# Layer 0's group steps behind their inputs, and norms by a power on GpSimd, in a four-layer graph network kernel

## The reference

```
L0: w = einsum(emb, weight);  out = sum_k T_k(adj) x w_k + emb bias
L1: h' = softmax(mask(adj > 0.5)) h;  out = elu(h')
L2: emb = x W' + b;  out = (adj + I) emb / deg
L3: three times  v = relu([v, adj v] W1' + b1) W2' + b2
x = layernorm(x + out)      # after each of the four
```

## Time and profile before

| | |
|---|---|
| median of 3 runs | 1052.36 us (1052.09 to 1052.92) |
| profiled execution | 1052.66 us, of it the profile's span 1050.9 us |
| PE busy | 1023.4 us (97%) |
| DVE / ACT / POOL busy | 690.4 / 453.4 / 538.1 us (66 / 43 / 51%) |
| granted PE clock | full, but for the last slice of 40 |
| first matmul, last matmul's end | 5.56 us, 1042.3 us |

### The profile page before, as it was taken

How to read it: one execution, slowest core, us unless ns; L and a number is a source line. 1 busy time by engine, 2 the same in 40 slices (tenths; PEclk the granted TensorE clock), 3 DMA queues, 4 the chain that set the end, 5 groups by cost and what they waited for, 6 DMA issues and landing times.

```text
span 1050.9 us, 18768 instructions
## 1 busy us (share of the span) xinstructions
PE 1023.4 (97%) x6922; PEld 490.9 (47%) x6922; DVE 690.4 (66%) x1728; ACT 453.4 (43%) x1097; POOL 538.1 (51%) x625
## 2 busy tenths in 40 slices
PE   7999999999999999999999999999999999999995
PEld 3445444434443444344345555555554545455553
DVE  3876565677547765775674778876546677767556
ACT  4632333333334343534423677557556622132632
POOL 0005486546456766775671757579764232223311
PEclk9999999999999999999999999999999999999998
DMA  9930000000000000000010121212112100000022
GB/s 365 400 128 1 2 1 2 1 2 1 1 1 2 1 1 2 1 1 2 1 41 1 41 81 41 81 41 80 53 69 81 41 1 1 3 2 21 22 61 61
DMA packets 14658, 45.66 MB, mean 43 GB/s; under 512 B 960, under 2 KB 9280, under 8 KB 10080
## 3 DMA queue, kind: packets, MB, share of 16 engines
q1 hardware_dynamic: 14560, 44.39, 11.4%
HBM read 40.19 MB, written 4.19 MB: 42 GB/s over the span
## 4 chain that ended last, share of the span: by engine, by line
PE 84%; DVE 9%; POOL 2%; ACT 2%; DMA 2%; issue 1%; SPq 0%; POOLq 0%; ACTq 0%; DVEq 0%
PE PS L750 34%; PE PS L880 21%; PE PS L924 18%; DMA BW<-at_in 2%; PE PS L735 2%; PE PS L737 2%; PE PS L736 2%; DVE BW L1200 1%; DVE T L1203 1%; DVE X L1203 1%; PE PS L744 1%; PE PS L742 1%; PE PS L743 1%; ACT T L1043 1%; PE PS L725 1%
## 5 line engine op out<-in xcount | busy, mean ns | idle before, releaser
L750 PE MATMUL PS<-BW,S 128*128 128x512 fp8e4 x1792 | 403.5, 379 | 4.3 <-POOL S L1708 1.9
L750 PEld LDWEIGHTS PS<-BW,S 128*128 128x128 f16 x1792 | 169.6, 98 | 211.0 <-issue 15.9
L1043 ACT ACTIVATE T<-PS,SM 128x128 f32<-128x128 f32 x384 | 112.5, 365 | 206.9 <-DVE X L1203 137.7
L880 PE MATMUL PS<-WZ,R 64*128 64x512 f16 x1536 | 198.5, 377 | 3.1 <-ACT T L1043 3.1
L1745 POOL TENSOR_TENSOR T<-T 128x128 f32<-128x128 f32 (+1 forms) x192 | 127.0, 662 | 124.9 <-ACT T L1043 114.4
L1203 DVE SCALAR_TENSOR_TENSOR X<-PS,SM,X 128x128 f32<-128x128 f32 x320 | 109.9, 344 | 38.7 <-PE PS L880 38.5
L880 PEld LDWEIGHTS PS<-WZ,R 64*128 64x128 f16 x1536 | 69.2, 94 | 106.8 <-issue 25.4
L924 PE MATMUL PS<-BW,S 128*128 128x512 fp8e4 x512 | 115.4, 379 | 0.4 <-issue 0.4
L1745 POOL TENSOR_TENSOR S<-R,S 128x512 f16<-128x512 f32 x48 | 57.5, 1210 | 94.2 <-ACT S L1043 94.2
L880 PE MATMUL PS<-WZ,T 64*128 64x512 f16 x768 | 103.8, 376 | 0.0
L1203 DVE SCALAR_TENSOR_TENSOR T<-PS,SM,T 128x128 f32<-128x128 f32 x256 | 88.0, 344 | 21.2 <-PE PS L880 21.2
(11 more groups left out here) (215 smaller groups left out, 1476.9 us busy)
## 6 DMA issues: line engine op xcount, KB each, us to landing
WZ<-a_in SPq DMA_DIRECT2D x16, 1024.0 KB, 4.8
BW<-at_in SPq DMA_DIRECT2D x8, 1024.0 KB, 18.3
R<-at_in SPq DMA_DIRECT2D x7, 1024.0 KB, 13.7
out<-X SPq DMA_DIRECT2D x16, 256.0 KB, 2.3
X<-x_in SPq DMA_DIRECT2D x3, 1024.0 KB, 20.3
T<-w_in SPq DMA_DIRECT2D x1, 1536.0 KB, 16.0
R<-at_in SPq DMA_DIRECT2D x2, 512.0 KB, 5.2
SM<-sm_in SPq DMA_DIRECT2D x1, 520.5 KB, 18.3
```

Of the source, the lines that this page charges most:

```text
L750: m = e.matmul(o, stile(h, t, c), Bm[:, t, block(j)], start=(t == 0 and h == 0), stop=(last and t == NT - 1 and h == 1))
L880: m = e.matmul(bank(b0 + q), halves[kd][zh][r, :], WZ[r, wh, kd, block(g)], start=(i == 0), stop=(i == 8))
L1043: return e.activation(o, i, f, **kw)
```

## The change

It does five things:

1. The group steps are placed by rounds counted through (`g` = 4u + t). `sq` is split into `sq` (ScalarE) and `red` (VectorE), with `red` a round or more behind. There are four buffers for the squares where layers 0 and 1 had one. `mean` goes from the second round of the unit after the group's norm to the second round of the unit after that, `addrow` and all behind it further on, for c = 3 into slots 2 to 11 of the last part (before: 0 to 7). The chains of `scales` are cut into six; two of them (`scales_b`, `scales_c`) go behind the middle.
2. `Z` is two steps, one a group, and on VectorE the low halves of `dx`, `E1`, `E2` and `E` 0 (`lo`) stand between the two groups of the following round. PE's order of `Z`, products, `dx` and `t1` stays.
3. In the head, `xs` 1 goes from before `P1` 2 to behind `t1` 3.
4. The weights' root: no Sqrt on ScalarE; GpSimd takes a maximum and a power of 0.5 right after its reduction over partitions, and VectorE waits for it.
5. The norms: no `var` on VectorE and no Sqrt; GpSimd adds epsilon and takes the power -0.5 of the sums (`var`, `var3`), 32 or 16 columns. `rs` on VectorE is four operations, one refining step, without the reciprocal.

```diff
-        + [("xs", 0), ("xs", 1)]
-        + pieces("P1", 2) + [("t1", 2), ("dx", 3), ("t1", 3), ("E1", 10), ("bounds",), ("xs", 2)]
+        + [("xs", 0)]
+        + pieces("P1", 2) + [("t1", 2), ("dx", 3), ("t1", 3), ("xs", 1), ("E1", 10), ("bounds",), ("xs", 2)]
...
+    for c in range(NC):
+        g = 16 * c
+        for j in range(4):
+            late = (c, j) == (3, 3)
+            at(g + 4 * j + (5 if late else 6), ("sq", 0, c, j))
+            at(g + 4 * j + (6 if late else 7), ("red", 0, c, j))
+        g += 16
+        if c < 3:
+            at(g + 3, ("var", 0, c))
+            at(g + 4, ("rs", 0, c), ("apply", 0, c, 0))
+            for j in (1, 2, 3):
+                at(g + 4 + j, ("apply", 0, c, j))
+            at(g + 7, ("sum", c))
+            g += 9
+            at(g, ("mean", c), ("row_a", c))
+            at(g + 1, ("row_b", c))
+            for j in range(4):
+                at(g + 2 + j, ("addrow", c, j))
+                at(g + 4 + j, ("sq", 1, c, j))
+                at(g + 5 + j, ("red", 1, c, j))
+            at(g + 8, ("var", 1, c))
+            for j in range(4):
+                at(g + 9 + j, *[("rs", 1, c)][j:], ("apply", 1, c, j), ("split", c, j))
...
     for k in range(5):
-        at(k // 2, 1 + 2 * (k % 2), ("xs", 3 + k))
-    at(2, 3, ("scales", 0))
-    at(3, 1, ("scales", 1))
-    at(3, 2, ("scales", 2))
+        at(2 * k + 1, ("xs", 3 + k))
+    at(9, ("scales", 0))
+    at(11, ("scales", 1))
+    at(13, ("scales", 2))
+    at(15, ("scales", 3))
+    at(65, ("scales", 4), ("scales", 5))
...
-            order += [("Z", u, t), ("add", u, t)]
-            order += after.pop((u, t), [])
+                if order[-1][0][0] == "E":
+                    lo.append(("lo", *order[-1]))
+
+            order += [("Z", u, t, 0), *lo, ("Z", u, t, 1), ("add", u, t)]
+            lo = []
+            order += after.pop(4 * u + t, [])
             if c < 3 and j < 2:
                 v = 4 * (c + 1) + 2 * j + t // 2
                 order.append(("dx" if t % 2 == 0 else "t1", v))
-        order += after.pop((u, 4), [])
+                if t % 2 == 0:
+                    lo.append(("lo", *order[-1]))
...
-                elif jt == 10:
-                    e.wait_ge(s_wsqr, 1)
-                    fn(col(cT3), col(cT3), ACT.Sqrt).then_inc(s_wroot, 1)
...
-                    e.wait_ge(s_wroot, 1)
-                    vc(ts(e, col(cZ), col(cT3), 1e-30, 1.0 / 1024, ALU.max, ALU.mult))
+                    e.wait_ge(s_wsqr, 3)
+                    vc(ts(e, col(cZ), col(cT3), 1.0 / 1024, None, ALU.mult))
...
-                    fc(e.reciprocal(s1, s1))
-                    fc(e.tensor_tensor(s0, s1, s1, ALU.mult))
-                    fc(e.tensor_tensor(s0, s0, s2, ALU.mult))
-                    fc(ts(e, s0, s0, -0.5, 1.5, ALU.mult, ALU.add))
-                    e.tensor_tensor(s2, s1, s0, ALU.mult).then_inc(s_rs, 1)
+                    m, eps = norm_scale(L)
+                    fc(e.tensor_tensor(s2, s1, s1, ALU.mult))
+                    fc(stt(e, s2, s0, eps, s2, ALU.add, ALU.mult))
+                    fc(ts(e, s2, s2, -0.5 * m ** 0.5, 1.5 * m ** 0.5, ALU.mult, ALU.add))
+                    e.tensor_tensor(s2, s1, s2, ALU.mult).then_inc(s_rs, 1)
...
             e.partition_all_reduce(col(cT3), wst[:, 0:1], 128, RED.max).then_inc(s_wsqr, 1)
+            e.wait_ge(s_wsqr, 1)
+            e.tensor_scalar(col(cT3), col(cT3), 1e-36, None, ALU.max).then_inc(s_wsqr, 1)
+            e.wait_ge(s_wsqr, 2)
+            e.tensor_tensor(col(cT3), col(cT3), col(cHalf), ALU.pow).then_inc(s_wsqr, 1)
...
+                elif kind in ("var", "var3"):
...
+                    s0, s1 = (st_part(L, c, j, k, 2 if L == 3 else 1) for k in range(2))
+                    pc(e.tensor_scalar(s1, s0, norm_scale(L)[1], None, ALU.add))
+                    e.tensor_tensor(s1, s1, col(cHalf + 1).broadcast_to(list(s1.shape)), ALU.pow).then_inc(s_pw, 1)
```

More of the change, by code:

```diff
@@ L31 @@
 cSG, cISG, cKG = 36, 40, 44
+cHalf = 46
 cF = 50
@@ L100, in at @@
-    def at(u, t, *steps):
-        after.setdefault((u, t), []).extend(steps)
+    after, rest = {}, {}
+    def at(g, *steps):
+        (after if g < 64 else rest).setdefault(g if g < 64 else g - 64, []).extend(steps)
     for c in range(NC):
+        g = 16 * c
         for j in range(4):
[L105 to L120, removed]
@@ L121, in middle_order @@
-    order = []
-    for k in range(5):
-        at(k // 2, 1 + 2 * (k % 2), ("xs", 3 + k))
-    at(2, 3, ("scales", 0))
-    at(3, 1, ("scales", 1))
-    at(3, 2, ("scales", 2))
+            late = (c, j) == (3, 3)
[18 more added lines that the diff above has]
+                at(g + 9 + j, *[("rs", 1, c)][j:], ("apply", 1, c, j), ("split", c, j))
+        else:
+            at(g + 2, ("var", 0, c))
+            at(g + 3, ("rs", 0, c), ("apply", 0, c, 0), ("apply", 0, c, 1))
+            at(g + 4, ("apply", 0, c, 2), ("apply", 0, c, 3), ("sum", c))
+            at(g + 6, ("mean", c), ("row_a", c))
+            at(g + 7, ("row_b", c))
+            for j in range(4):
+                at(g + 7 + j // 3, ("addrow", c, j))
+                at(g + 8 + j // 3, ("sq", 1, c, j))
+                at(g + 9, ("red", 1, c, j))
+            at(g + 9, ("var", 1, c))
+            for j in range(4):
+                at(g + 10 + j // 2, *[("rs", 1, c)][j:], ("apply", 1, c, j), ("split", c, j))
@@ L156, in at @@
         late.setdefault(k, []).extend(steps)
-    for (u, t) in sorted(after):
-        at(u - 16, *after[u, t])
+    for k in sorted(after):
+        at(k, *after[k])
     for c in range(NC):
@@ L1054, in scalar_steps @@
                     act_e2(e, step[1])
-                elif kind == "scales" and step[1] == 0:
+                elif kind == "scales" and step[1] == 1:
                     e.wait_ge(s_xc, NT)
@@ L1404, in scales_c @@
                 e.wait_ge(s_sc, 1)
-                for t in range(2):
-                    e.wait_ge(s_hh, 2 + t)
-                    stt(e, hat[:, 1, t:4:2, :], BD[:, t::2, :], cs[:, cRho64 + t:cRho64 + t + 1], hat[:, 0, t:4:2, :],
-                        ALU.mult, ALU.subtract).then_inc(s_hl, 1)
             for step in steps:
                 kind = step[0]
-                if kind == "E1":
-                    dve_e1(e, step[1])
+                if kind == "lo" and step[1] == "E1":
+                    dve_e1(e, step[2])
+                elif kind == "lo" and step[1] == "E2":
+                    dve_e2(e, step[2])
+                elif kind == "lo" and step[1] == "dx":
+                    dve_dx(e, step[2])
+                elif kind == "lo":
+                    e.wait_ge(s_zh, 1)
+                    lo_half(e, T[:, 0, 1, block(0)], bank(product_bank(0)), T[:, 0, 0, block(0)], s_zl)
@@ L1524, in vector_steps @@
                     ts(e, ROW[:, 0, :], ROW[:, 0, :], LAM, None, ALU.mult).then_inc(s_row, 1)
-                elif kind == "E":
+                elif kind == "E" and step[1] > 0:
                     k = step[1]
```

193 lines of the change are left out of this document (94 added, 99 removed).

## The result

| kernel | median | range | against before, 95% interval |
|---|---|---|---|
| before, beside it | 1052.82 us | 1052.09 to 1053.16 (5) | |
| changed | 1099.02 us | 1098.08 to 1099.79 (5) | 1.044 [1.0428, 1.0453] |

A forecast was written before the change was run, and what follows sets the result against it. TensorE, busy 97% of the span, was taken to bound the kernel, so only its waits counted. -8.7 + 7.4 - 0.3 + 2.1 + 0.3 = +0.8 on the profiled 1052.66, with the median 0.3 lower: 1053.2 us, range 1046.0 to 1058.5.

The forecast's parts named there:

- part 2: `lo` between a round's two groups: low halves release PSUM banks 0.29 us late for TensorE's next products, +7.4 us.
- part 4: Head: the root by GpSimd's power waits for its code to reload, delaying VectorE and then TensorE, +2.1 us.
- part 5: Norms: power taken as 1.3 us for 32 columns, 0.8 for 16, hidden in the middle, exposed at the end; +0.3 us.
- (d): Rival, norms: the power is slow and decides from 3 us on; 1057.2 at 4 us, near 1070 at 7; chance 0.15.
- Part 1: Group steps placed later in middle and last part: TensorE's seven gaps for ScalarE, VectorE and the mean go, -8.7 us.
- rival (e): Last part: layer 1's later steps meet GpSimd's mask differences and hold back product 12; 2 to 3 us, 1056; chance 0.10.
- 20 to 30: Sign of being right: that many short TensorE waits for VectorE's low halves, 0.1 to 0.2 us idle each.
- Part 3: Head, `xs` 1 later: GpSimd's 1.9 us wait goes, but TensorE waits in the third round; -0.3 us kept.
- The end: After VectorE's last sum, the last norm's power and four operations stand before the output: 1.67 us grows, +0.4 us.

The follow-up runs named there:

- e2: e1 with the `lo` halves ahead of the round again (changed order, roots on ScalarE): 1050.33 us, 0.9975 of the kernel before.
- e1: Changed kernel with its order kept but every root, head and norms, back on ScalarE's Sqrt, no power: 1054.85 us, 1.0023 of the kernel before.
- e11: Changed kernel with only the `lo` halves ahead of the round's first group again; power kept for head and norms: 1094.91 us, 1.0398 of before.
- e3: Changed kernel with only the head's root back on ScalarE; norms keep GpSimd's power: 1095.99 us, 1.0414 of the kernel before.
- e5: e2 plus five unread GpSimd powers of 1 to 64 columns and one multiplication before GpSimd's first all-reduce: 1051.67 us, executed once.
- e6: e2 plus GpSimd powers of the same size at each norm's place, results unread, norms using ScalarE's roots: 1057.22 us, 1.0048 of before.
- e7: Changed kernel with head's root on ScalarE, `lo` halves ahead, groups 0 to 2 one round later from `rs` on: 1086.33 us, 1.0311 of before.
- e9: e2 with layer 1's mean, row, squares and applies of the last column group one slot earlier, one apply per slot: 1048.52 us, 0.9962 of before.
- e12: e9 with the head's `xs` 1 back ahead of the third product's pieces, as before the change: 1048.56 us, 0.9961 of the kernel before.

## Why the prediction was wrong, step by step

| term | predicted | measured | from |
|---|---|---|---|
| parts 1 and 3, order | -9.0 | -2.1 | e2 - before |
| part 2, `lo` halves | +7.4 | +4.5, +4.1 | e1 - e2; changed - e11 |
| part 4, head's root | +2.1 | +3.0 | changed - e3 |
| part 5, norms | +0.3 | +41.1 | e3 - e1 |

-2.1 + 4.5 + 3.0 + 41.1 = 46.5. That this is the whole loss is no evidence: each difference starts where another ends, so that they must add up to it. e11, which isn't in this chain, supports the second. By the intervals each is uncertain by 1 to 1.5 us.

**Part 5 failed**, and twice over. The first step is "I take 1.3 us for 32 columns and 0.8 for 16, nearer the additions, since it runs as the same kind of instruction". It takes 5.53 and 2.95. I had bounds from 0.27 to 6.93 and no row between; the nearness of the kind of instruction was no evidence on its arithmetic, and e5 shows it. It is one of the signs of being wrong that I had named, "if the power takes more than 3 us". The kernel's own price by the column was off by a factor of some 75: about 2.1 ns for an addition (from the earlier trace rows, 1018 ns for 384 columns and 483 for 128), about 160 ns for a power. By the Trainium skill ("GPSIMD Engine Reference", 3.1 Elementwise — side-by-side cycle accounting) a GpSimd operation on two tensors takes some 2.6 cycles of a 1.2 GHz clock an element, which is 2.2 ns. The trace agrees for the additions. By an estimate from that figure of the page a power of 32 columns would be 0.07 us on top of its start, and the rows say 5.5, so the figure doesn't carry over to the power.

The second step is the rival that had the right mechanism. (d) said that the power decides from 3 us on, that "at 4 us, two places with a `lo` right behind lose 1.4 each and the end 1.2 more", and near 1070 at 7 us. By its own working (two places, the length above a slack of 2.6 us, and 2.2 at the end) the measured 5.5 us gives 1061; at 7 us it gives 1065, and the 1070 has no working. The kernel took 1099. Three things were missing. First, I counted two places. VectorE stood in 19, and the last part, which I had not looked at for this, lost 20.0 us: VectorE's longest wait, 6.49 us up to 661.27, is there, the whole of an addition and a power. Second, a stall of VectorE isn't only its excess over a slack of 2.6: everything queued behind `rs` comes late together, and 4.03 us there made 5.08 on TensorE. Third, the clock. The longest waits bring TensorE back at its lower level, 1.0 us for a product each time and an estimated 12 us in all. No term of the sum and no rival had it, because the kernel before has no wait over 2 us in the middle and a clock of 1.00. That VectorE's `rs` waits are the larger part, e6 shows: GpSimd's time for the same powers is worth 6.9 us, which leaves some 34 of the 41.1 for the waits on the results, if the two add up. In the last part GpSimd's time cost nothing in e6, so the loss there is the waits'. In the middle it is mixed: GpSimd's time alone is 9.1 us, and e7 gets only 5.8 back by asking a round later, because once VectorE doesn't wait, ScalarE does. How the middle's loss splits between the two stays open.

**Part 1** gains 2.1 with part 3 and not 9.0. It named seven gaps, and all are gone: no wait for the row and none for ScalarE's copies in e2 but that of the third round. What failed is its last sentence, that "the cover of the moved steps is VectorE's and ScalarE's slack in rounds of about 6 us". With the halves ahead and ScalarE's roots the middle is 4.0 us shorter (417.1 against 421.1), 5.9 without the third round's wait. The rest went into three new waits for VectorE's low halves, 0.28, 1.32 and 0.79 us, 2.8 with the hidden gaps. The last part is 4.7 us longer (271.1 against 266.4): three waits of 2.6 us in all, 3.0 with the hidden gaps, and an estimated 1.7 by the clock behind them. e9 takes 2.4 of the 4.7 back. This is rival (e) near its place and price (2 to 3 us), but TensorE waits for VectorE, not for GpSimd, and GpSimd's differences are in it at most by making an operation of VectorE longer.

**Part 2** had its mechanism right. A round of the changed kernel, TensorE, then VectorE, which answers to the earlier trace rows:

```profile
195.53 0.82 PE L915 MATMUL PS<-WZ,R 64*128 64x512 f16 x6
...
199.80 1.90 PE L787 MATMUL PS<-BW,S 128*128 128x512 fp8e4 x8 [0.20 <-DVE R L1229]
...
199.06 0.68 DVE L1229 SCALAR_TENSOR_TENSOR R<-PS,R 128x512 f16<-128x512 f32 x1
```

The next product starts 4.27 us after the round, 0.28 more than 3.99; I had 0.29. The size was off. The list of the changed kernel has seven waits of 0.20 or 0.21 us, the last of them at 223.36, not the 20 to 30 that I had named as a sign. Between e1 and e2 the middle differs by 5.5 us (422.6 and 417.1) where I had 7.4, that is 19 places of 0.29 instead of 30. The last part gives 1.6 back (269.5 against 271.1), although TensorE has the same three waits there in both: it goes with the clock, which fell in e2's profiled execution and not in e1's. Which of the places don't pay I didn't sort out.

**Part 3** was right, in mechanism and size. The wait of 1.9 left the head and 1.6 to 1.9 came back in the third round, behind the same pause of GpSimd; e12 measured 0.04 us for the exchange, where I had 0.3, and the two can't be told apart.

**Part 4** was right, its size 0.9 short, which is within that uncertainty. GpSimd, then VectorE, which answers to the earlier trace rows:

```profile
44.83 0.25 POOL L1756 TENSOR_SCALAR cs<-cs 128x1 f32<-128x1 f32 x1 [7.03 <-issue]
45.17 0.60 POOL L1758 TENSOR_TENSOR cs<-cs 128x1 f32<-128x1 f32 x1
...
45.80 0.34 DVE L1221 TENSOR_SCALAR cs<-cs 128x1 f32<-128x1 f32 x2 [2.45 <-POOL cs L1758]
```

GpSimd went on at 44.83 (I had 44.9), and VectorE went on at 45.80 against 43.45 before, 2.35 later (I had 2.1). The first embedding product is at 110.4 in the changed kernel and at 107.6 in e3, so the delay reaches TensorE whole.

**The end** of the page, which I priced at 0.4: VectorE's sum ends at 1089.30, its output operation starts at 1093.60 behind GpSimd's power of 16 columns, 4.30 us where the earlier trace rows have 1.67. That is +2.6, by a power of 2.92.

```profile
1087.84 1.46 DVE L1232 TENSOR_REDUCE T<-WZ 128x8 f32<-128x512 f32 x2
1092.77 0.17 DVE L1515 TENSOR_TENSOR T<-T 128x16 f32<-128x16 f32 x1 [3.46 <-POOL T L1822]
...
1093.60 1.49 DVE L1242 TENSOR_TENSOR X<-X,T 128x512 f32<-128x512 f32 x2
```

## What to carry to other kernels

An operation that no row shows can't be priced by its kind of instruction; here it was 18 times its neighbour. Where its bounds are 0.3 and 7 us and twenty of them stand on a chain, that one number is the forecast, and the range must reach as far as the upper bound times the places, in all stages. A wait in an in-order engine is paid by all that is queued behind it, and asking later helps only as far as nothing else is queued behind the slow operation on its own engine. Two kernels that differ by 1 or 2 us may differ by one fall of the clock, so look at the granted clock of each stretch before giving the difference to an edit. Before a step is moved, add up what the receiving rounds hold already for each engine.

## What was not expected of the hardware

- GpSimd's power: 0.60, 1.90, 2.99, 5.68 and 10.62 us for 1, 8, 16, 32 and 64 columns, against 0.31 us for a multiplication of 32.
- TensorE's granted clock after a wait: a mean of 0.61 and 0.60 in the 3.7 us behind waits of 5.08 and 6.43 us, with 1.00 after them; behind a wait of 1.28 us (at 265.90) and one of 2.61 (at 671.69) it stayed at 1.00. Behind 0.57, 0.97 and 1.01 us within 12 us it fell in e2 and not in e1, so the length of the last wait doesn't tell.
- VectorE's smallest operations are longer in places where GpSimd works. In e2, four operations of `rs` on 32 columns, while GpSimd adds and multiplies on two tensors without a break from 362.73 to 369.07:

```profile
364.73 0.88 DVE L1539 TENSOR_TENSOR T<-T 128x32 f32<-128x32 f32 x1
365.64 1.08 DVE L1239 SCALAR_TENSOR_TENSOR T<-T 128x32 f32<-128x32 f32 x1
366.76 0.91 DVE L1232 TENSOR_SCALAR T<-T 128x32 f32<-128x32 f32 x1
367.70 0.19 DVE L1542 TENSOR_TENSOR T<-T 128x32 f32<-128x32 f32 x1
```

The first three take 4.6 to 5.7 times as long as the last, which lies beside GpSimd's operations too. Later in e2, at 622.35 to 625.79, all four take 1.02 to 1.20 us while GpSimd works without a break; the four in the kernel before, at 623.85 to 624.52, take 0.18 or 0.19 each while GpSimd stands idle (619.90 to 632.42). By the Trainium skill ("GPSIMD Engine Reference", 8. Key points) GpSimd shares its interfaces to SBUF with VectorE and contends with VectorE's operations on two SBUF inputs. The rows agree for 364.73 and 365.64, but not for the `TENSOR_SCALAR` of 0.91 us, unless it counts as one of the two-port mode that the page names beside them, and not for 367.70. What tells these apart wasn't tried.
